# A gated linear-attention block and a 12-expert layer in one launch: the turn of x behind the turn of the keys in odd chunks, and five smaller edits of order and count

## The chip, the cores and the metric

The kernel runs on one core of one Trainium2 chip. The time is the device time of one execution in microseconds (us); the profile is of one execution of the same program on that core.

## What is computed

The reference, cut to what matters (the reshapes, the type conversions and the drawing of the inputs are left out):

```
# x: (1, 2048, 512) float32; 8 heads of 64
xn = layernorm(x, gamma, beta)
w = sigmoid(xn @ Wx @ Ww + bw); k = xn @ Wk; v = xn @ Wv; r = sigmoid(xn @ Wr)
for t in range(2048):                       # per head
    state = (1 - w[t])[:, None] * state + k[t][:, None] * v[t][None, :]
    y[t] = r[t] @ state
x = layernorm(x + y @ Wo)
p = softmax(x @ gate_w.T); top 2 of 12 experts, their weights made to sum to 1
x = layernorm(x + sum over the two experts of weight * (silu(x @ w1.T) * (x @ w3.T)) @ w2.T)
```

Every product of the dense layers is made of float16 high and low parts, three matmuls for one.

## The kernel before

Each engine runs an instruction list that is written out by hand; semaphores tie the lists together. There are two blocks, `attention` and `experts`.

**attention.** The 2048 tokens are 16 chunks of 128 (`NT`), two of which make a pair `q` (`NPAIR` = 8). The projections of a pair are ten jobs (`job` on TensorE, `take` on ScalarE): 0 and 1 turn the normalised x (line 358, eight transposes for both), 2 and 3 make the decay z, 4 and 5 the key, 6 and 7 the receptance, 8 and 9 the value. They share the two banks of `pA`, so job number i of `SEQUENCE` waits until take number i-2 is done. After the two takes of the turned x, ScalarE makes its float16 high part (`high_x`, line 794) and VectorE its low part (`low_x`, line 1055), and the jobs from 2 on need both.

Inside a chunk the recurrence is a tree of seven levels. For the chunk that comes next, VectorE multiplies the receptance side (`dve_level`, lines 715, 716 and 724) and POOL the key side (`pool_level`, line 740), while ScalarE copies the halves that stay (`act_receptance`, line 670, here `rec_levels`; `act_key`, line 683, here `key_levels`). Receptance level 6 on VectorE needs ScalarE's `rec_levels(5)`. For the present chunk TensorE makes `scores` half 0 (line 394), VectorE puts them through masks into `ST[0]` (`mask`, lines 1070 and 1073), and TensorE applies them to the values (`apply_values`, line 419); the same follows for half 1, where VectorE's `mask` half 1 stands behind levels 1 to 6 in its list. `read_state` (405) reads the carried state, `turn_keys` (429) turns the keys into `pM`, ScalarE copies that to `kbT` (902), and `attend_out` (454 to 456), the output projection of the chunk before, writes into the same `pM` and so waits for the copy.

Odd chunks 1 to 11 run with the slots `FIRST`, even ones from 2 on with `SECOND`, chunk 0 with `ZEROTH`. A `FIRST` chunk starts a new pair: ScalarE's `normalise` (800) makes the rows that jobs 0 and 1 turn. In TensorE's list its order is scores half 0, jobs 0 and 1, `read_state`, `turn_keys`, `attend_out`, `apply_values` half 0. In ScalarE's list it is `normalise`, the first levels, takes 0 and 1, the copy to `kbT`, `high_x`, further levels, `rec_levels(4)`, then `fill(0)`, the take of job 2, and behind it `rec_levels(5)`.

Beside all this the expert weights are split into float16 parts for the second block, in 48 pieces. `PIECES[n]` says how many are handled with the levels of chunk n, that is during chunk n-1: ScalarE makes the high part (`act_piece`, 691), POOL the low part (`pool_piece`, 746), and SP's queue moves them in and out through two buffers. The fourth piece of a chunk is the last thing in ScalarE's list of the chunk before, ahead of its `normalise`.

**The prologue** loads everything on SP's queue. TensorE runs six matmuls on a zeroed tile (572), then Wx @ Ww (576), the turns and the first jobs in the order of `START`. The weights of the output projection come last; ScalarE makes their high part in two halves (987, 1000) and POOL the low part (`low_out`, 1276), the second half behind the key levels of chunk 0.

**experts.** A routing part counts and ranks the tokens. In it TensorE keeps itself at work with matmuls on the identity (`busy`, line 1502), the last group of which has 21 and runs until VectorE has the routing tables and weights ready (line 1762). Then come 43 tiles of gathered tokens through `turn` (1537), `hidden` (1556 to 1558), `turn_hidden` (1564) and `down` (1574 to 1577), and a last part that adds and normalises.

## Time and profile before

| | |
|---|---|
| median of 3 runs | 780.29 us (778.42 to 787.46) |
| the profiled execution's own time | 779.44 us |
| its span, first to last instruction | 777.6 us |
| TensorE matmul busy | 736.8 us (95%), 6367 instructions |
| VectorE busy | 492.3 us (63%) |
| ScalarE busy | 347.4 us (45%) |
| POOL busy | 306.3 us (39%) |
| mean granted TensorE clock | 0.991 of full speed |

In the span, attention runs to about 460 us, routing to about 480 us, the tiles of the experts to about 744 us and the last part to the end. The rows further down are of four views. The waits say which engine an engine waited for. A timeline lists an engine's instructions in order of time: start, duration, engine, line, operation, output<-inputs, partitions and elements, how many were merged, and in square brackets the idle time before them with what ended it. A table of stretches gives busy time by engine with the clock. TensorE's matmuls overlap: in a merged row the last one's end is modelled and reaches about 0.16 us over the start of the next.

### The profile page before, as it was taken

The numbers are of one execution on the slowest core, as the hardware profiler recorded it, in microseconds if no ns is written. First come the engines' busy times: TensorE is split into PE (matmuls) and PEld (weight loads), VectorE is DVE, ScalarE is ACT, GpSimd is POOL, SyncE is SP. The second block draws the span as 40 slices with busy tenths as digits, with TensorE's granted clock in tenths as the row PEclk, the third lists the DMA queues.
The fourth block names the chain that finished last, engine by engine and source line by source line (L and its number), as shares of the span: only waits on it lengthen the run. The fifth ranks groups of instructions, "written<-read, shape, count | busy, mean of one in ns | idle before, by whom it ended". The sixth has DMA issues, their size and how long they took to land. (4 is left out here: it accounts for less than half of the span.)

```text
span 777.6 us, 18216 instructions
## 1 busy us (share of the span) xinstructions
PE 736.8 (95%) x6367; PEld 542.9 (70%) x6368; DVE 492.3 (63%) x1102; ACT 347.4 (45%) x695; POOL 306.3 (39%) x336
## 2 busy tenths in 40 slices
PE   9999899999999999999999988999999999999994
PEld 4778678787878777877867777666666666666641
DVE  3857868768586687785868876444444444444477
ACT  3865654556456566576465211222222222222264
POOL 0564555554554544655512002233443434334310
PEclk9999999999999999999999999999999999999998
DMA  9833455343552454537311026355355555532855
GB/s 333 295 101 118 142 184 164 113 158 112 184 179 74 163 164 146 172 124 236 112 43 41 28 74 235 141 203 188 131 217 217 211 198 200 189 94 81 326 231 199
DMA packets 40124, 126.79 MB, mean 163 GB/s; under 512 B 4224, under 2 KB 4608, under 8 KB 38144
## 3 DMA queue, kind: packets, MB, share of 16 engines
q1 hardware_dynamic: 31024, 99.49, 36.8%
q0 software_dynamic: 6880, 22.55, 8.6%
q10 hardware_dynamic: 2160, 3.93, 1.4%
q8 instruction: 40, 0.66, 0.4%
q14 instruction: 20, 0.16, 0.1%
HBM read 81.13 MB, written 44.83 MB: 162 GB/s over the span
## 5 line engine op out<-in xcount | busy, mean ns | idle before, releaser
L1070 DVE COPY_PREDICATED ST<-msk,pS 128x256 f32<-128x256 uint8 x224 | 121.2, 569 | 66.9 <-issue 37.7
L746 POOL TENSOR_TENSOR piece_parts<-piece,piece_parts 128x1024 f16<-128x1024 f32 x48 | 104.1, 2170 | 109.5 <-ACT piece_parts L691 109.5
L1556 PE MATMUL pH<-ring,xgh 128*128 x344 | 103.7, 301 | 3.9 <-issue 2.7
L740 POOL TENSOR_TENSOR L<-L,AM 128x256 f32<-128x256 f32 x96 | 73.0, 761 | 79.4 <-ACT L L683 70.9
L1557 PE MATMUL pH<-ring,xgh 128*128 x344 | 103.4, 301 | 0.0
L1558 PE MATMUL pH<-ring,xgl 128*128 x344 | 103.3, 300 | 0.0
L1868 POOL DMA_INDIRECT y_scratch<-ysb,sidx x43 | 42.9, 997 | 138.5 <-DVE ysb L1785 138.5
L394 PE MATMUL pS<-L 64*128 64x64 f32 x1536 | 96.2, 271 | 0.0
L1769 DVE TENSOR_TENSOR hid<-pH,sil 128x320 f32<-128x320 f32 x43 | 21.1, 492 | 118.3 <-ACT sil L1640 90.2
L394 PEld LDWEIGHTS pS<-L 64*128 64x128 f32 x1536 | 91.1, 188 | 0.0
L724 DVE TENSOR_TENSOR L<-L,AM 128x256 f32<-128x256 f32 x96 | 65.8, 686 | 26.2 <-ACT L L670 24.3
L1640 ACT ACTIVATE sil<-pH 128x320 f32<-128x320 f32 x43 | 18.8, 438 | 129.6 <-PE pH L1558 129.6
L369 PE MATMUL pA<-xh,early 128*128 128x256 f16 x256 | 69.8, 273 | 1.5 <-ACT val L788 1.1
L371 PE MATMUL pA<-xh,early 128*128 128x256 f16 x256 | 69.8, 273 | 0.0
L370 PE MATMUL pA<-xl,early 128*128 128x256 f16 x256 | 69.8, 273 | 0.0
L691 ACT CAST piece_parts<-piece 128x1024 f16<-128x1024 f32 x48 | 50.2, 1045 | 27.9 <-DMA piece<-in_w_experts 27.9
L1855 POOL DMA_INDIRECT xg<-x_scratch,gidx x39 | 39.0, 999 | 31.0 <-POOL gidx L1852 22.8
L1574 PE MATMUL pO<-ring,hTh 128*128 x129 | 49.0, 380 | 1.4 <-DVE hTh L1780 1.4
L1556 PEld LDWEIGHTS pH<-ring,xgh 128*128 128x128 f16 x344 | 33.7, 98 | 22.7 <-issue 10.0
L1636 ACT CAST hTh<-pHT 128x384 f16<-128x384 f32 x43 | 20.6, 479 | 63.4 <-PE pHT L1564 63.4
L1575 PE MATMUL pO<-ring,hTh 128*128 x129 | 48.9, 379 | 0.0
L1785 DVE COPY ysb<-pO 128x512 f32<-128x512 f32 x43 | 29.8, 692 | 22.9 <-PE pO L1575 20.4
(256 smaller groups left out, 1596.3 us busy)
## 6 DMA issues: line engine op xcount, KB each, us to landing
piece<-in_w_experts SPq DMA_DIRECT2D x48, 512.0 KB, 5.1
w_split_scratch<-piece_parts SPq DMA_DIRECT2D x48, 512.0 KB, 3.9
ring<-w_split_scratch SPq DMA_DIRECT2D x12, 2048.0 KB
yin<-y_scratch SPq DMA_DIRECT2D x16, 512.0 KB, 11.1
out_x<-X SPq DMA_DIRECT2D x8, 512.0 KB, 2.8
x_scratch<-X ACTq DMA_DIRECT2D x15, 256.0 KB, 2.0
X<-in_x SPq DMA_DIRECT2D x2, 1536.0 KB, 18.4
wxT_sb<-in_wxT SPq DMA_DIRECT2D x4, 256.0 KB, 4.9
```

The lines of the kernel that those rows point to most:

```text
L369: pe.matmul(o, wh[name][:, kt, cols], xh[par][:, kt, :], start=(kt == 0), stop=False)
L370: pe.matmul(o, wh[name][:, kt, cols], xl[par][:, kt, :], start=False, stop=False)
L371: i = pe.matmul(o, wl[name][:, kt, cols], xh[par][:, kt, :], start=False, stop=(kt == KT - 1))
L394: i = pe.matmul(o, k_, r_, start=True, stop=True)
L691: a.copy(piece_parts[buf][:, 0, :], piece[buf][:, :]).then_inc(piece_hi, 1)
L724: v.tensor_tensor(next_grown(k, lv, 1), grown(rec, k, lv, 1), factor(c, lv, 0), ALU.mult).then_inc(r_dec, 1)
L740: g.tensor_tensor(next_kept(k, lv, 0), kept(key, k, lv, 0), by, ALU.mult).then_inc(k_dec, 1)
L746: g.tensor_tensor(piece_parts[buf][:, 1, :], piece[buf][:, :], piece_parts[buf][:, 0, :], ALU.subtract).then_inc(piece_lo, 1)
L1070: v.copy_predicated(out[:, :, :, 0 if lv == 0 else 1, :], msk[:, lv, :, :].rearrange(shape, m=m), pS[:, :, lv * S:(lv + 1) * S].rearrange( ...
L1556: pe.matmul(p[:, 0, 0:F], xgh[par][:, k, :], wh, start=(k == 0), stop=False)
L1557: pe.matmul(p[:, 0, 0:F], xgh[par][:, k, :], wl, start=False, stop=False)
L1558: t = pe.matmul(p[:, 0, 0:F], xgl[par][:, k, :], wh, start=False, stop=(k == KT - 1))
```

## The change

There are six edits.

1. In `FIRST` chunks TensorE turns x (jobs 0 and 1) behind `read_state` and `turn_keys` instead of ahead of them, and ScalarE's takes 0 and 1 stand behind the copy to `kbT`.
2. In the same chunks ScalarE's `rec_levels(5)` stands ahead of `fill(0)`.
3. The zero matmuls at the start are 4 instead of 6.
4. The second half of the output weights' low part is made by VectorE behind chunk 0's receptance levels instead of by POOL behind its key levels; the semaphore `wo_lo` becomes two. In the prologue's ScalarE list `take(0, 8, 0)` stands two places further ahead.
5. `PIECES[1]` is 3 instead of 4 and `PIECES[5]` is 4 instead of 3.
6. The last `busy` of the routing part has 29 matmuls instead of 21.

```diff
@@ -51,7 +51,7 @@
 HALVES_OF = ((0, 1), (2, 3))
 GROUP = 4
 PIECE_AT = {4: (0,), 5: (1,), 6: (2, 3)}
-PIECES = [2, 4] + [4 if n % 2 == 0 else 3 for n in range(2, NT - 2)] + [0, 0]
+PIECES = [2, 3] + [4 if n % 2 == 0 or n == 5 else 3 for n in range(2, NT - 2)] + [0, 0]
 
 
 TOP = NL - 1
@@ -238,7 +238,7 @@
         y_out = sem("y_out")
         y_low = sem("y_low")
         wo_hi = sem("wo_hi")
-        wo_lo = sem("wo_lo")
+        wo_lo = [sem(f"wo_lo{i}") for i in range(2)]
         m_full = sem("m_full")
         kb_out = sem("kb_out")
         sd_ready = sem("sd_ready")
@@ -439,7 +439,8 @@
                 i.then_inc(m_full, 1)
 
             def attend_out(n):
-                pe.wait_ge(wo_lo, 2)
+                for i in range(2):
+                    pe.wait_ge(wo_lo[i], 1)
                 pe.wait_ge(y_out, n + 2)
                 pe.wait_ge(y_low, n + 2)
                 if n == NT - 1:
@@ -528,13 +529,13 @@
                 pe.wait_ge(k_dec, n * NL + (NL - 1))
                 pe.wait_ge(k_kept, n * (NL - 1) + (NL - 1))
                 scores(n, k, 0)
-                if slots is FIRST:
-                    job(q, 0, par)
-                    job(q, 1, par)
                 gating(0)
                 read_state(n, k)
                 if n < NT - 1:
                     turn_keys(n, k)
+                if slots is FIRST:
+                    job(q, 0, par)
+                    job(q, 1, par)
                 gating(1)
                 if slots is not FIRST:
                     fill(0)
@@ -568,7 +569,7 @@
                 fill(3)
 
             pe.wait_ge(zeroed, 1)
-            for i in range(6):
+            for i in range(4):
                 pe.matmul(pY[:, 0, :], state[:, 0, :], state[:, :, :].rearrange("p k t -> p (k t)"), start=True, stop=True)
             for kt in range(KT):
                 pe.wait_ge(wz_in[kt], 32)
@@ -762,7 +763,8 @@
                 bank, half = order(q, m) % 2, m % 2
                 a.wait_ge(a_full, order(q, m) + 1)
                 if q == 1 and (m == 6 or m == 8):
-                    a.wait_ge(wo_lo, 2)
+                    for i in range(2):
+                        a.wait_ge(wo_lo[i], 1)
                 if n is not None and m == 4:
                     a.wait_ge(s_full, n * 2 + 2)
                 if m < 2:
@@ -888,10 +890,7 @@
                 key_levels(0)
                 rec_levels(1)
                 key_levels(1)
-                if slots is FIRST:
-                    take(q, 0, par)
-                    take(q, 1, par)
-                else:
+                if slots is not FIRST:
                     early_norms()
                 if n == 0:
                     root(2, 7)
@@ -901,6 +900,8 @@
                     a.wait_ge(m_full, n * 3 + 1)
                     a.copy(kbT[:, :], pM[:, 0, :]).then_inc(kb_out, 1)
                 if slots is FIRST:
+                    take(q, 0, par)
+                    take(q, 1, par)
                     high_x(q, par)
                 if n == NT - 3:
                     a.wait_ge(x_lo, NPAIR)
@@ -931,11 +932,13 @@
                 split(0)
                 rec_levels(4)
                 if slots is FIRST:
+                    rec_levels(5)
                     if n == 9:
                         root_x1(0)
                     early_norms()
                     fill(0)
-                rec_levels(5)
+                else:
+                    rec_levels(5)
                 gating(4)
                 late_norms(4)
                 split(1)
@@ -1001,9 +1004,9 @@
             act_key(a, 0, 0, 0, 5)
             act_receptance(a, 0, 0, 1)
             act_receptance(a, 0, 0, 2)
+            take(0, 8, 0)
             act_receptance(a, 0, 0, 3)
             act_receptance(a, 0, 0, 4)
-            take(0, 8, 0)
             act_receptance(a, 0, 0, 5)
             act_piece(a, 0, 0, 0)
             take(1, 2, 1)
@@ -1248,6 +1251,8 @@
             dve_decays(v, 0, 0, 0)
             for lv in range(NL):
                 dve_level(v, 0, 0, 0, lv)
+            v.wait_ge(wo_hi, 2)
+            v.tensor_tensor(wo_l[:, 2:4, :], wo_stage[1], wo_h[:, 2:4, :], ALU.subtract).then_inc(wo_lo[1], 1)
             chunk(0, 0, nxt=0)
             for j in range((NPAIR - 2) // 2):
                 for u in range(2):
@@ -1271,10 +1276,6 @@
 
         @block.gpsimd
         def _(g):
-            def low_out(i):
-                g.wait_ge(wo_hi, i + 1)
-                g.tensor_tensor(wo_l[:, 2 * i:2 * i + 2, :], wo_stage[i], wo_h[:, 2 * i:2 * i + 2, :], ALU.subtract).then_inc(wo_lo, 1)
-
             g.wait_ge(stat1, 6)
             for i, name in ((1, "r"), (2, "v")):
                 g.wait_ge(w_hi, i + 1)
@@ -1283,9 +1284,9 @@
             for name in "krv":
                 g.wait_ge(w_lo[name], 1)
             g.wait_ge(wz_full, KT)
-            low_out(0)
+            g.wait_ge(wo_hi, 1)
+            g.tensor_tensor(wo_l[:, 0:2, :], wo_stage[0], wo_h[:, 0:2, :], ALU.subtract).then_inc(wo_lo[0], 1)
             pool_chunk(g, 0, 0, 0)
-            low_out(1)
             for t in range(PIECES[0]):
                 pool_piece(g, 0, 0, t)
             pool_chunk(g, 1, 1, 0)
@@ -1525,7 +1526,7 @@
             for n in range(NT, 2 * NT):
                 t = pe.matmul(pH1[:, 0, 0:SLOTS], ro.oh_col[:, n, :], oh_tile[:, n, :], start=(n == NT), stop=(n == 2 * NT - 1))
             t.then_inc(second_full, 1)
-            busy(21)
+            busy(29)
 
 
             def turn(i, k, rounds):
```

TensorE's list in a `FIRST` chunk, from the last scores of half 0 to the first of the output projection. The rows of before (358 is the turn of x, 405 `read_state`, 429 `turn_keys`, 454 to 456 `attend_out`):

```order
L394 MATMUL pS<-L 128x64 x12
L358 MATMUL pA<-idt,pair_x 128x128 x8
L405 MATMUL pY<-L,state 128x128 x4
L429 MATMUL pM<-idt,L 128x128 x4
L454 MATMUL pM<-wo_h,yTh 128x512
```

and of the changed kernel, where the output projection is line 455:

```order
L394 MATMUL pS<-L 128x64 x12
L405 MATMUL pY<-L,state 128x128 x4
L429 MATMUL pM<-idt,L 128x128 x4
L358 MATMUL pA<-idt,pair_x 128x128 x8
L455 MATMUL pM<-wo_h,yTh 128x512
```

The eight transposes of x have moved from ahead of the read to between the keys' turn and the output projection.

ScalarE's list in the first `FIRST` chunk, chunk 1, from a piece of the expert weights to the second take of z. The rows of before (800 is `normalise`, 773 the takes of x, 902 the copy to `kbT`, 794 the high part, 784 the takes of z, 670 the receptance levels, the last of which is `rec_levels(5)`):

```order
L691 CAST piece_parts<-piece 128x1024
L800 ACTIVATE pair_x<-X,nmr,rstd 128x512 x2
L683 COPY L<-key 128x256
L670 COPY L<-L 128x128x2
L683 COPY L<-L 128x128x2
L773 ACTIVATE pair_x<-pA,vecs 128x256 x4
L902 COPY kbT<-pM 128x512
L794 CAST xh<-pair_x 128x1024
...
L670 COPY L<-L 128x16x16
L784 ACTIVATE dec<-pA,neg_bw 128x2x128 x2
L670 COPY L<-L 128x4x2x32
```

and of the changed kernel (950 is the copy of y that stood ahead of the fourth piece before):

```order
L950 CAST yTh<-pY 128x512
L802 ACTIVATE pair_x<-X,nmr,rstd 128x512 x2
L684 COPY L<-key 128x256
L671 COPY L<-L 128x128x2
L684 COPY L<-L 128x128x2
L901 COPY kbT<-pM 128x512
L775 ACTIVATE pair_x<-pA,vecs 128x256 x4
L796 CAST xh<-pair_x 128x1024
...
L671 COPY L<-L 128x16x16
L671 COPY L<-L 128x4x2x32
L786 ACTIVATE dec<-pA,neg_bw 128x2x128 x2
```

The fourth piece is gone from ahead of `normalise`, the copy to `kbT` has passed the takes of x, and the last receptance copy has passed the take of z.

## Rows read from the trace of the kernel before

**Rows 1.** The waits of TensorE: line, who ended it, total, times, longest.

```profile
PE pM L454 <- ACT kbT L902: 5.6, 7, 1.2
PE pY L419 <- DVE ST L1073: 5.0, 11, 0.7
```

**Rows 2.** Timeline of TensorE in chunk 7, a steady odd chunk.

```profile
235.26 1.09 PE L358 MATMUL pA<-idt,pair_x 128*128 128x128 f32 x8
237.08 0.60 PE L429 MATMUL pM<-idt,L 128*128 128x128 f32 x4
238.50 0.38 PE L454 MATMUL pM<-wo_h,yTh 128*128 128x512 f16 x1 [0.82 <-ACT kbT L902]
...
241.19 0.66 PE L419 MATMUL pY<-ST,val 128*64 128x128 f32 x8
...
254.92 0.66 PE L419 MATMUL pY<-ST,val 128*64 128x128 f32 x8 [0.50 <-DVE ST L1073]
```

**Rows 3.** Timeline of VectorE in chunk 7.

```profile
240.03 0.42 DVE L1073 COPY ST<-pS 64x256 f32<-64x256 f32 x1
...
249.56 0.43 DVE L724 TENSOR_TENSOR L<-L,AM 128x256 f32<-128x256 f32 x1 [2.98 <-ACT L L670]
...
254.45 0.42 DVE L1073 COPY ST<-pS 64x256 f32<-64x256 f32 x1
```

**Rows 4.** Timeline of ScalarE in chunk 7.

```profile
235.95 1.93 ACT L773 ACTIVATE pair_x<-pA,vecs 128x256 f32<-128x256 f32 x4 [1.34 <-PE pA L358]
237.77 0.59 ACT L902 COPY kbT<-pM 128x512 f32<-128x512 f32 x1
238.23 1.07 ACT L794 CAST xh<-pair_x 128x1024 f16<-128x1024 f32 x1
```

**Rows 5.** Timeline of TensorE in chunk 1.

```profile
80.56 1.39 PE L358 MATMUL pA<-idt,pair_x 128*128 128x128 f32 x8 [1.94 <-ACT pair_x L800]
...
85.70 0.38 PE L454 MATMUL pM<-wo_h,yTh 128*128 128x512 f16 x1 [1.19 <-ACT kbT L902]
...
88.39 0.66 PE L419 MATMUL pY<-ST,val 128*64 128x128 f32 x8
```

**Rows 6.** Timelines of ScalarE, VectorE and POOL ahead of chunk 1's first mask.

```profile
77.95 1.04 ACT L691 CAST piece_parts<-piece 128x1024 f16<-128x1024 f32 x1 [2.42 <-DMA piece<-in_w_experts]
78.90 1.51 ACT L800 ACTIVATE pair_x<-X,nmr,rstd 128x512 f32<-128x512 f32 x2
...
79.47 2.02 DVE L715 TENSOR_TENSOR L<-rec,dec 128x256 f32<-128x256 f32 x1
81.41 1.06 DVE L716 TENSOR_TENSOR L<-rec,AM 128x256 f32<-128x256 f32 x1
...
79.07 2.14 POOL L746 TENSOR_TENSOR piece_parts<-piece,piece_parts 128x1024 f16<-128x1024 f32 x1 [2.48 <-ACT piece_parts L691]
```

**Rows 7.** Table of stretches: busy by engine, PEclk, DMA share, GB/s.

```profile
80.00:85.00 5.00, 3.95 (x20) 3.58 (x20) 4.71 (x6) 3.23 (x9) 3.61 (x4) 0.66 0.68 221
...
480.00:485.00 5.00, 5.00 (x28) 3.61 (x28) 0.69 (x1) 1.87 (x2) 0.00 (x0) 0.66 1.02 383
```

**Rows 8.** The page's DMA issues: KB each, median us to landing.

```profile
piece<-in_w_experts SPq DMA_DIRECT2D x48, 512.0 KB, 5.1
```

**Rows 9.** Timeline of TensorE in the prologue, first matmul of two runs of jobs.

```profile
30.68 0.27 PE L369 MATMUL pA<-xh,early 128*128 128x256 f16 x1 [0.35 <-ACT pair_x L773]
...
47.67 0.28 PE L369 MATMUL pA<-xh,early 128*128 128x256 f16 x1 [1.15 <-ACT val L788]
```

**Rows 10.** Timelines of ScalarE and POOL in the prologue.

```profile
34.78 0.84 ACT L784 ACTIVATE dec<-pA,neg_bw 128x256 f32<-128x256 f32 x2
...
44.11 2.31 POOL L1276 TENSOR_TENSOR wo_l<-rec,wo_h 128x1024 f16<-128x1024 f32 x1
```

**Rows 11.** Timeline of TensorE at the end of the routing part.

```profile
472.27 4.93 PE L1502 MATMUL pH<-idt 128*128 128x128 f32 x42
479.48 0.63 PE L1537 MATMUL pA<-idt,xg 128*128 128x128 f32 x4 [2.27 <-DVEq L1762]
```

## The prediction

> **What bounds the kernel now.** The table of the profile says that TensorE is busy for 95% of the span, so I looked for the few moments at which it is not. The waits of TensorE come first [rows 1]. 5.6 us in 7 waits stand ahead of the output projection and end with ScalarE's copy to kbT; 5.0 us in 11 waits stand ahead of applying the scores and end with VectorE's mask. Next I read the timeline of a steady odd chunk, chunk 7. There TensorE has two holes [rows 2]: 0.82 us ahead of line 454 and 0.50 us ahead of the second line 419. Chunks 3, 5, 9 and 11 repeat them, even chunks have neither. Then I read the other engines at these two places [rows 3, 4], and last the places where the holes are larger: chunk 1 [rows 5 to 7], the prologue [rows 9, 10] and the end of routing [rows 7, 11]. Everything between them is TensorE at full pace, which the change leaves as it is. So the sum is over holes.
>
> **Edit 1, the turn of x, in chunks 3, 5, 7, 9 and 11.** Before, ScalarE is in the takes of x from 235.95 for 1.93 us, to 237.88, and only then makes the copy to kbT [rows 4], although the keys' turn began at 237.08 and ended at 237.68 [rows 2]. TensorE starts line 454 at 238.50. In the new order TensorE reaches the keys' turn earlier by the turn of x: 1.09 us, less the overlap of 0.16, is 0.93. The keys' turn ends at 236.75, ScalarE is free, the copy takes 0.59 and is done at 237.4, while TensorE turns x until 237.6. Line 454 can start at about 237.55, which is 0.95 us earlier. All of it can't be kept: the next thing, line 419, needs VectorE's mask half 0, which starts when the scores are there, and those do not move. That mask ends at 240.03 + 0.42 = 240.45 [rows 3]; VectorE to TensorE takes 0.05 (254.87 to 254.92, [rows 2, 3]). So line 419 starts at 240.50 instead of 241.19: **0.69 us** a chunk. The bounds are 0 and 0.95.
>
> The takes of x are what is late now. They run from 237.35 to 239.3, the high part (1.07) to 240.2 or 240.3 instead of 239.30 [rows 4]. VectorE comes to the low part when the mask is done, at 240.37. The slack is 0.1 to 0.2 us; each 0.1 more would push levels 1 to 6 by 0.1. Behind `high_x` on ScalarE stand the key levels 2 and 3, for which POOL waits, and everything there comes about 0.9 us later. I cost this at nothing, since VectorE has a hole of 2.98 us before its last level [rows 3], which edit 2 opens.
>
> **Edit 2, `rec_levels(5)` ahead of the take of z.** VectorE's level 6 waited 2.98 us for a copy of 0.4 us that stood behind a take which waits for TensorE's z job. Now that copy follows `rec_levels(4)` directly; level 6 can run at about 247, when level 5 is done, and the mask of half 1 starts then instead of at 249.9. Even with 0.9 us lost to edit 1 it is done more than 1 us before TensorE comes to the second line 419. The hole of 0.50 goes: **0.57 us** with the overlap of 0.07 that adjacent matmuls have there. The bounds are 0 and 0.57.
>
> Five chunks at 0.69 + 0.57 = 1.26 are **6.3 us**.
>
> **Chunk 1, edits 1, 2 and 5.** Here ScalarE waits 2.42 us for the transfer of a fourth piece and splits it, then normalises x from 78.90 on [rows 6], and TensorE sits 1.94 us ahead of the turn of x [rows 5]. The same piece on POOL, 79.07 to 81.21, stretches VectorE's level 0 to 2.02 + 1.06 us; elsewhere these two take 0.42 each, pitched 0.33, so VectorE is ready for the mask at 82.47 instead of about 80.2. On top of that the granted clock falls: 0.66 over 80 to 85 [rows 7], and the turn of x takes 1.39 instead of 1.09 [rows 2, 5]. Without the piece normalise is done before TensorE asks. VectorE then bounds the chunk: level 0 ready at 80.2 (in the times of before), 4.9 us of mask (249.97 to 254.87 in chunk 7, [rows 3]), 0.3 left for POOL's first key level beside it, and line 419 at about 85.45 instead of 88.39. That is **2.9 us**, and 0.55 for the second mask as above, **3.5 us**. TensorE still sits about 0.8 us twice in it, which is less than either idle time after which the clock fell. Bounds: 1.9 (the wait for normalise alone) and 4.5: from the end of the scores, 80.56 - 1.94 = 78.62, to line 419 it is 9.77 us here, and would be 240.50 - 235.26 = 5.24 in a steady chunk [rows 2, 5].
>
> **The rule for two engines at one memory.** VectorE's line 715 starts at 79.47, POOL's piece ends at 81.21, and line 715 ends at 81.49 [rows 6]: not slowed but held until the piece is through. The Trainium skill, "SBUF — State Buffer", section "Who interferes with whom", says this: a VectorE instruction with two inputs in SBUF and a GpSimd instruction share one port pair, the first to start has it to its end, and the other waits in full. The trace agrees, with 0.28 us between the two ends.
>
> That speaks against edit 5, since chunk 5 now has the fourth piece. There the load is issued once the second piece is through, takes 5.1 us [rows 8], and POOL's work of 2.14 us falls on the same level 0. Chunk 4 has the even chunk's longer lead, and I find level 0 ready for chunk 5's mask within 0.2 us of the scores: **-0.2 us**, bounds 0 and -3.
>
> **Prologue, edits 3 and 4.** TensorE sits 1.15 us at 47.67 for the take of the value [rows 9], 1.31 with the overlap of 0.16. That take stood behind receptance copies which VectorE delayed, and VectorE was held by POOL's second half of the low part, 44.11 to 46.42 [rows 10]. Both are moved: the take comes two copies earlier, and the low part (about 1.2 us on VectorE, like the low part of x of the same size) falls between the levels and the mask, where VectorE has nothing to do. All **1.3 us** come back; bounds 0 and 1.3. Two zero matmuls fewer are 1.7 us at the pace of the last ones, but it does not last: job (0, 6), the third of the run from 30.68, needs the take (0, 2), which ends at 34.78 + 0.84 = 35.62 [rows 9, 10] behind a cast that waits for the transfer of the output weights. TensorE came there at about 35.9. So **0.3 us**, bounds 0 and 1.7.
>
> **End of routing, edit 6.** 42 records in 4.93 us are 0.117 each [rows 11]; a matmul is two, so 8 more are 1.9 us, inside the hole of 2.27. They delay nothing, 0.4 us of idle stays. The gain is the clock: after the hole it was 0.66 over 480 to 485 [rows 7]. At 1.2 instead of 2.4 GHz for part of the stretch, 5 x (1 - 0.66) = 1.7 us are lost; some 0.4 of it falls on fill matmuls that hide behind ScalarE's and VectorE's parts of the first tile. **1.3 us**, bounds 0 and 1.7.
>
> **The sum.** 6.3 + 3.5 - 0.2 + 1.3 + 0.3 + 1.3 = 12.5 us. From the profiled execution's 779.44 that gives 766.9, say **767.0 us**, and a span near 765.1. The median of the three runs is 0.85 above the profiled execution, within their own scatter.
>
> **Rivals.**
>
> *The odd chunks keep their second hole.* POOL's pieces, later by 0.9 us, hold VectorE's levels, or the late high part of x does, and the mask of half 1 ends no earlier than TensorE's arrival. Against it: 2.98 us of room. For it: the slack of 0.1 to 0.2 at the low part. Six chunks lose 0.57: 767.0 + 3.4 = 770.4.
>
> *The fourth piece does in chunk 5 what it did in chunk 1.* For it: the same two instructions meet, and a level 0 that is held until the piece is through passes its whole delay to the mask. Against it: a transfer that starts earlier against TensorE. It costs up to 3 us and perhaps the clock: 770 to 771. (By the rule of the Trainium skill, "SBUF — State Buffer", section "Who interferes with whom", POOL's piece would be first here and VectorE held in full; the hold in rows 6 agrees.)
>
> *The turns uncover a wait, and it is slower.* Before, the turn of x gave 0.93 us between the scores and the read of the state and the keys' turn. If the last key level of POOL or the state were that late, TensorE would sit in each odd chunk. To be slower at all this must cost more than 12.5 / 6 = 2.1 us a chunk; at 2.5 it would be 782. Against it: in even chunks the read follows the scores directly, and line 405 has no entry among TensorE's waits.
>
> *The gains don't add, no change.* If the masks of half 0 alone bounded the odd chunks and moved with the copies on ScalarE, edits 1 and 2 would give nothing, and 12.5 - 6.9 = 5.6 us would be left: 773.8.
>
> **How the numbers follow.** The forecast has 0.60; either of the first two rivals 0.22; no change in the odd chunks 0.09; the slower one 0.03; 3 us more than forecast (VectorE freer in chunk 1 than I count, the prologue at its bound) 0.06. The range reaches from 763.5 (chunk 1 and the prologue at their upper bounds) to 771.5, which takes in the first two rivals. 1% is 7.8 us, about what a measurement of this kernel can tell: faster than 772.5 us 0.86, within 1% 0.11, slower 0.03; 0.02 of the first two rivals I count within 1%, for the scatter.
>
> **What would show it.** In the changed profile TensorE's waits for kbT should fall from 5.6 us in 7 to under 1.5 us, in chunks 1 and 14 alone; line 419's first application in each odd chunk should follow the mask's copy by 0.05 us with a hole near 0.1, the second should have none; VectorE's hole of 2.98 ahead of level 6 should be gone; the clock should read 1.0 in chunk 1 and after routing; the wait at 47.67 should be gone, and one of up to 1.1 us should appear ahead of job (0, 6). The prediction is wrong if `low_x` waits for the high part by more than 0.3 us, if chunk 5 shows a late mask, or if the clock falls at a place where it did not before.

## The result and the profile after

The changed kernel takes 774.71 us, the median of 13 runs (771.47 to 777.42); beside it on the same chip the kernel before takes 780.29 us (778.05 to 787.46, 13 runs). The ratio is 0.9914, with a 95% interval of 0.9887 to 0.9941. So it is faster, by 0.9%, where 1.7% was forecast, and the time is outside the range. The profiled execution took 777.42 us with a span of 775.5 and was the slowest of the 13; the profiled execution of before, 779.44, was one of its better ones (4 of its 13 runs were faster). That matters below.

The waits of TensorE in the changed kernel, to be read against [rows 1] (line 455 is the output projection, 405 the state's read):

```profile
PE pY L419 <- DVE ST L1076: 3.3, 7, 0.9
PE pY L405 <- issue: 2.2, 1, 2.2
PE pA L369 <- ACT dec L786: 1.8, 1, 1.8
...
PE pM L455 <- DVE yTl L1192: 1.0, 1, 1.0
...
PE pA L1538 <- DVEq L1763: 0.5, 1, 0.5
...
PE pM L455 <- ACT kbT L901: 0.3, 1, 0.3
```

The 5.6 us for kbT are 0.3, those for the mask 3.3 instead of 5.0. Two waits are new: 2.2 us ahead of the state's read and 1.8 ahead of a job. (The 1.0 us for yTl, the low part of y, is at the end of chunk 15, where the kernel before has a wait of 1.0 us at its line 501.)

Chunk 7 in the changed kernel, TensorE, against [rows 2]:

```profile
230.31 1.16 PE L405 MATMUL pY<-L,state 128*128 128x128 f32 x8
231.31 0.60 PE L429 MATMUL pM<-idt,L 128*128 128x128 f32 x4
231.74 1.04 PE L358 MATMUL pA<-idt,pair_x 128*128 128x128 f32 x8
232.67 0.38 PE L455 MATMUL pM<-wo_h,yTh 128*128 128x512 f16 x1
...
235.63 0.62 PE L419 MATMUL pY<-ST,val 128*64 128x128 f32 x7 [0.21 <-DVE ST L1076]
...
248.80 0.44 PE L419 MATMUL pY<-ST,val 128*64 128x128 f32 x4
```

VectorE and ScalarE beside it, against [rows 3, 4]:

```profile
235.07 0.42 DVE L1076 COPY ST<-pS 64x256 f32<-64x256 f32 x1
235.47 1.23 DVE L1058 TENSOR_TENSOR xl<-pair_x,xh 128x1024 f16<-128x1024 f32 x1
...
240.75 2.15 DVE L725 TENSOR_TENSOR L<-L,AM 128x256 f32<-128x256 f32 x2
242.83 4.49 DVE L1073 COPY_PREDICATED ST<-msk,pS 128x256 f32<-128x256 uint8 x7
...
231.94 0.59 ACT L901 COPY kbT<-pM 128x512 f32<-128x512 f32 x1 [2.29 <-PE pM L429]
232.43 1.94 ACT L775 ACTIVATE pair_x<-pA,vecs 128x256 f32<-128x256 f32 x4
234.39 1.04 ACT L796 CAST xh<-pair_x 128x1024 f16<-128x1024 f32 x1
```

The copy to kbT now waits for TensorE, not for the takes, and TensorE goes into line 455 with no hole. The high part of x ends at 235.43, the mask at 235.49: VectorE comes to the low part 0.06 us after it is there. Level 6 follows level 5 directly (two in 2.15), the idle time of 2.98 us is gone, and the second line 419 has no hole. In chunk 7 everything stands as forecast, but for 0.21 us instead of about 0.1 ahead of the first line 419.

The stretches make it plain where the program stands. The numbers are us from the first scores of a chunk to those of another, from the timelines of TensorE, in the two profiles and in a second profile of each kernel (the experiments tell of them); the first row and the last are a time from the span's start and the whole span:

```
                               before   changed   changed, 2nd   before, 2nd
first scores of chunk 0         53.02     51.59       51.83          53.73
chunk 1                         30.55     29.09       28.23          32.09
chunks 3, 5, 7, 9, 11          133.31    128.14      127.86         133.31
chunks 13 and 14                46.51     48.15       46.51          46.51
chunk 15 to the routing part    31.31     37.00       37.00          36.44
first to second tile of x        6.54      5.45        5.45           6.49
span                            777.6     775.5       773.2          786.6
```

Up to chunk 13 the changed kernel is 8.0 us ahead (384.39 against 376.40). Then it loses 1.6 us in chunks 13 and 14 and 5.7 in chunk 15, where the two programs are the same instruction by instruction. The stretches of the changed kernel show why (columns as in [rows 7]):

```profile
100.00:390.00 290.00, 287.05 (x3044) 229.84 (x3042) 220.01 (x398) 173.37 (x348) 151.49 (x124) 1.00 0.48 154
390.00:400.00 10.00, 10.00 (x96) 8.52 (x94) 7.38 (x15) 4.80 (x11) 1.46 (x2) 0.83 0.16 58
400.00:430.00 30.00, 28.77 (x330) 22.15 (x329) 23.91 (x91) 15.38 (x36) 4.06 (x6) 1.00 0.10 37
430.00:456.00 26.00, 24.11 (x188) 21.59 (x187) 16.25 (x63) 3.61 (x9) 0.00 (x0) 0.74 0.06 21
```

The granted clock, 1.00 over the 290 us of steady chunks, was at its lower level (1.2 GHz) for part of 390 to 400 and for half of 430 to 456. So 7.3 us went to the clock in a part of the program that the change doesn't touch.

### The profile page after: what moved, and what is told of

It reads as the page before. It is cut to its first block and busy times, and to the rows that moved or that the text cites. A ratio compares the mean times of both kernels' runs of the same rounds, so it can differ in the third digit from the quotient of the medians.

```text
span 775.5 us, 18242 instructions
## 1 busy us (share of the span) xinstructions
PE 742.6 (96%) x6379; PEld 551.1 (71%) x6380; DVE 501.4 (65%) x1103; ACT 347.9 (45%) x695; POOL 302.5 (39%) x335
## 5 line engine op out<-in xcount | busy, mean ns | idle before, releaser
L741 POOL TENSOR_TENSOR L<-L,AM 128x256 f32<-128x256 f32 x96 | 70.7, 736 | 84.1 <-ACT L L684 75.2
L394 PE MATMUL pS<-L 64*128 64x64 f32 x1536 | 98.8, 276 | 0.0
L394 PEld LDWEIGHTS pS<-L 64*128 64x128 f32 x1536 | 93.6, 193 | 0.0
L725 DVE TENSOR_TENSOR L<-L,AM 128x256 f32<-128x256 f32 x96 | 68.7, 716 | 11.3 <-ACT L L671 9.4
```

The source lines that it names most:

```text
L394: i = pe.matmul(o, k_, r_, start=True, stop=True)
L741: g.tensor_tensor(next_kept(k, lv, 0), kept(key, k, lv, 0), by, ALU.mult).then_inc(k_dec, 1)
```

## The experiments

The theories. **A**: the holes (idle times of TensorE) were worth what the trace up to chunk 13 shows; the clock falls at places that differ from one execution to the next, in either kernel, and one profile of each happened to differ. **B**: moving the turns makes the clock fall later on. **C**: the holes of 0.70 and 0.91 us in chunks 14 and 15 make it fall. **D**: the places belong to the instruction lists, and came with the change.

**The changed kernel again**, no edit.

> The changed kernel itself, a second time. Theory A (the clock falls at places that differ from one execution to the next, in either kernel): its profile shows low clock at other places than the first profile (chunk 1, chunks 13 and 15, the end), and its times spread over 5 us or more with the mean clock. Theory D (the places belong to the instruction lists): the same stretches again. At a like mean clock it should be some 8 us below the kernel before.

Measured: 774.59 us (772.58 to 777.24, 7 runs) against 784.08 us (23 runs of before on that chip), ratio 0.9893 (0.9854 to 0.9932). Its profile:

```profile
74.00:90.00 16.00, 13.10 (x169) 10.97 (x168) 14.50 (x25) 11.10 (x25) 7.08 (x7) 1.00 0.26 90
...
390.00:400.00 10.00, 10.00 (x111) 7.98 (x110) 7.91 (x23) 5.89 (x12) 1.04 (x2) 1.00 0.22 80
...
430.00:456.00 26.00, 24.11 (x188) 21.68 (x186) 16.00 (x66) 3.17 (x8) 0.00 (x0) 0.74 0.06 21
```

The clock held in chunk 1 and in chunk 13, where it had fallen in the first profile of the same program, and fell in chunk 15 again. With the clock held chunk 1 takes 28.23 us instead of 29.09. The times spread over 4.7 us, a little less than A asked for.

**The kernel before again**, no edit.

> The kernel before, profiled a second time. Theory A: its first profile, at a mean clock of 0.991 and 779.44 us, was one of its better executions, and an execution of ordinary clock (0.984 to 0.986) shows stretches of low clock in the gating chunks 13 to 15 as the changed kernel does, with an end 4 to 6 us later than 779.4. Theory D (the low clock in chunks 13 to 15 came with the change): nothing under 1.0 between 85 and 460 us, and about 779.

Measured: 788.41 us at a mean clock of 0.978 (one execution), and in its profile:

```profile
74.00:90.00 16.00, 12.05 (x106) 8.62 (x105) 14.92 (x24) 10.87 (x22) 8.74 (x7) 0.79 0.60 189
100.00:390.00 290.00, 282.90 (x3016) 227.51 (x3015) 212.90 (x395) 165.81 (x332) 151.69 (x121) 1.00 0.47 152
390.00:440.00 50.00, 47.62 (x505) 35.98 (x504) 39.07 (x125) 28.93 (x65) 7.95 (x12) 1.00 0.10 38
440.00:465.00 25.00, 23.62 (x183) 20.95 (x182) 15.56 (x62) 3.18 (x8) 0.00 (x0) 0.73 0.06 22
465.00:480.00 15.00, 13.53 (x110) 12.35 (x108) 11.73 (x49) 2.07 (x3) 0.00 (x0) 0.89 0.43 159
```

The kernel before loses the clock in chunk 15 too (36.44 us to the routing part, against 37.00 in the changed kernel), and also in the routing part, where neither profile of the changed kernel does. This is one execution, 9.0 us above the profiled one on which the prediction was built, where 4 to 6 were expected, and it settles D: the low clock of chunk 15 did not come with the change. Of the 14 profiles of all kernels here, the clock held all through chunk 15 in two (31.3 and 31.7 us to the routing part), it was low for 3.4 us in three (31.7 to 32.3), and for 6.8 to 13.7 us in nine (33.8 to 37.0). In eight of these nine, kernels of either order among them, it fell 14 to 16 us behind the chunk's first scores. So A is right in that no execution need have the fall, but the place is not at random: chunk 15 is where it comes most. In chunk 13 it fell in one profile of the 14, the first of the changed kernel.

**A measure at a like clock.** Every run has its mean granted clock. In the 60 runs of before that stood beside the experiments it goes from 0.977 to 0.994, and the time from 788.92 to 776.87 with it. One slope fits all kernels, 0.59 us for 0.001 of mean clock (fitted within kernels). With it each kernel's mean is put at a clock of 0.985:

```
                                runs   mean clock   mean us   at 0.985   error
before                            60      0.9851     783.46     783.5     0.1
changed (first chip)              13      0.9855     774.79     775.1     0.3
changed, again                     7      0.9867     774.72     775.7     0.5
edits 1 and 2 alone                4      0.9892     773.58     776.1     0.3
edit 1 alone                      10      0.9906     777.17     780.5     0.3
edit 2 alone                      10      0.9870     779.11     780.3     0.3
edits 3 to 6 alone                10      0.9860     782.49     783.1     0.2
changed, pieces as before         10      0.9847     776.94     776.8     0.3
changed, six zero matmuls          9      0.9868     774.84     775.9     0.2
changed, pad before chunk 13       5      0.9858     775.41     775.9     0.5
changed, late fill                 4      0.9872     773.68     775.0     0.5
changed, low y ahead               4      0.9885     773.65     775.7     0.3
low y ahead, six zero, late fill   6      0.9932     770.50     775.3     0.4
```

At a like clock the change is worth 7.8 us beside the runs of before of the same chip, and 8.4 by the runs of the first chip; the runs of before that stood beside those have no clock on record. The last column is the scatter of the runs alone. The correction is a fit, and a fall of the clock doesn't cost the same everywhere: 3.4 us at the lower level in chunk 15 made the way to the routing part 0.4, 0.5 and 1.0 us longer in three profiles. It also takes the mean clock as given, which an edit could itself move. Where a trace has the stretch itself, I use the trace.

**Edits 1 and 2 alone.**

```diff
                 scores(n, k, 0)
-                if slots is FIRST:
-                    job(q, 0, par)
-                    job(q, 1, par)
                 gating(0)
                 read_state(n, k)
                 if n < NT - 1:
                     turn_keys(n, k)
+                if slots is FIRST:
+                    job(q, 0, par)
+                    job(q, 1, par)
                 gating(1)
```

(with the takes and `rec_levels(5)` moved as in the change)

> The kernel before with the two edits of order alone (turn of x behind the keys' turn, last receptance copy ahead of the take of z). In the trace of the changed kernel the five odd chunks 3 to 11 gave 1.17, 0.87, 1.16, 0.81 and 1.06 us, 5.1 together, and chunk 1 may give 0.5 to 1 more. Theory A (the holes are worth what the trace shows, and what is missing in the whole is the clock of chunks 13 and 15, which depends on when the program comes to them): attention reaches the start of chunk 13 about 5.5 us earlier than before; the time is 773.5 to 775 if the clock holds in chunks 13 to 15 and up to 8 us more if it falls. Theory B (moving the turns makes TensorE's later work itself slower, wherever it lies): the clock falls in chunks 13 and 15 at the same instructions as in the changed kernel.

Measured: 772.44 us (771.01 to 778.42, 4 runs) against 784.17 (14 runs), ratio 0.9881 (0.9828 to 0.9933). In the trace the five steady odd chunks take 25.48 to 25.50 each, against 26.66: 1.17 us a chunk, 5.9 in all. Chunk 1 takes 29.10. At a like clock 7.4 of the 7.8 us are here. Attention reaches chunk 13 at 377.47, 6.9 us before the first profile of before, where 5.5 were expected. B would have the clock fall where it did in the changed kernel; it held in chunk 13 and fell for 3.4 us in chunk 15, later in the chunk.

**Edits 3 to 6 alone** (the changed kernel with the order taken back).

> The changed kernel with the two edits of order taken back: prologue, pieces and routing fill alone. Theory A: chunk 0 starts 1.4 us earlier, chunk 1 gives about 1.5 more, the routing fill 1.1; with the clock held in chunks 13 to 15 that is 775 to 776, up to 8 us more if it falls. Theory B: the clock never falls in chunks 13 to 15, since the turns are where they were.

Measured: 782.85 us (777.86 to 784.98, 10 runs) against 784.17 (14 runs), ratio 0.9990 (0.9961 to 1.0019), so no gain can be told from none. B falls here: with the turns in their old place the clock fell in chunk 15 all the same (36.95 us to the routing part). The prologue's gain was lost in this profile: TensorE waited 2.23 us ahead of job (0, 6), the clock was low over 36 to 40 us, and chunk 0 started at 53.76, no earlier than before. At a like clock the four edits together give 0.4 us, with an error of 0.2: much less than the 2 to 3 us that the prologue, chunk 1 and the first tile show together in the traces of the changed kernel. The experiment on the pieces, below, shows a part of the reason.

**Edit 1 alone.**

> The kernel before with the turn of x moved behind the keys' turn, alone. In the trace: TensorE's wait for kbT in the steady odd chunks goes from 0.82 us to nothing, a hole of 0.1 to 0.2 us stands ahead of line 419's first application, and the second hole of 0.5 us stays, since level 6 is still behind the take of z: 0.6 to 0.7 us less for each of the chunks 3 to 11. At a like clock 4 to 5 us below the kernel before.

Measured: 777.22 us (774.65 to 779.83, 10 runs) against 782.84 (23 runs), ratio 0.9930 (0.9896 to 0.9964). The steady odd chunks take 26.04 to 26.08 us: 0.61 less. The trace has the hole ahead of the first application that was expected:

```profile
139.97 0.66 PE L419 MATMUL pY<-ST,val 128*64 128x128 f32 x8 [0.21 <-DVE ST L1072]
```

Chunk 1 gains nothing by this edit alone: it takes 31.27 us, with a hole of 3.17 us ahead of the state's read and a fall of the clock at it.

**Edit 2 alone.** `rec_levels(5)` ahead of `fill(0)` in the kernel before.

> The kernel before with the last receptance copy ahead of the take of z, alone. In the trace: VectorE's idle time of 3 us ahead of level 6 goes, and TensorE's hole of 0.5 us ahead of line 419's second application with it: 0.57 us less for each of six odd chunks, the wait for kbT stays at 0.82. At a like clock 3 to 3.5 us below the kernel before.

Measured: 777.14 us (776.24 to 785.04, 10 runs) against 782.84 (23 runs), ratio 0.9945 (0.9905 to 0.9984). The steady odd chunks take 26.09 or 26.10 us: 0.56 less. In the steady odd chunks the two edits add up, 0.61 + 0.56 = 1.17, as in the kernel with both. At a like clock they are 3.0 us, where 4 to 5 were expected, and 3.2: together 6.2, against 7.4 for the kernel with both. In the traces the missing 1.2 us are chunk 1, which takes 31.27 us with edit 1 alone, 30.41 with edit 2 alone and 29.10 with both, against 30.55 and 32.09 before.

**A pad ahead of chunk 13.**

```diff
+                if n == NT - 3:
+                    pe.wait_ge(s_dve, n * 2 + 1)
+                    busy(pS[:, 0, :], 4)
                 scores(n, k, 0)
```

> The changed kernel with 4 more matmuls on the identity ahead of chunk 13's scores, 0.94 us; they change nothing before, and in chunks 13 to 15 only when the same work is done. Theory A (time of arrival): the stretches of low clock in chunks 13 and 15 move to other instructions, shrink, or go; total between 5 us faster and 3 us slower than the changed kernel. Theory B: they stay at the same instructions, and the time is the changed kernel's plus 0.9.

Measured: 777.04 us (771.15 to 777.87, 5 runs), ratio 0.9884 (0.9842 to 0.9926). The clock was low for 6.8 us in chunk 1, held in chunk 13, fell in chunk 15 (36.95 us to the routing part) and in the routing part (18.46 us instead of 17.25). Since the unpadded kernel held in chunk 13 too in its second profile, this says nothing of the moment of arrival: the experiment doesn't decide what picks the execution in which the clock falls.

**The late fills.**

```diff
                 gating(5)
+                if n == NT - 2:
+                    pe.wait_ge(gate_out, 18)
+                    busy(pA[:, 1, :], 3)
...
-                    busy(pA[:, 0, :], 10)
+                    busy(pA[:, 0, :], 14)
```

> The changed kernel with TensorE's holes late in chunk 14 and early in chunk 15 (0.70 and 0.91 us) filled by 3 and 4 more matmuls on the identity. If those holes make the clock fall behind them (theory C: less work just before the fall decides), the low stretch of 13.7 us in chunk 15 goes and the time falls by about 6 us to some 769 to 770. Theory A: it may stay or go, with no loss of more than 0.3 us from the fill itself.

Measured: 773.87 us (770.95 to 776.01, 4 runs), ratio 0.9883 (0.9843 to 0.9922). The profile held the clock in chunk 15, at a time of 770.95. But the other three runs have mean clocks of 0.983, 0.988 and 0.985, like the changed kernel's. C isn't shown; at a like clock the kernel is within the errors of the changed one (775.0), so the fill costs nothing that can be told.

**The pieces as before.**

```diff
-PIECES = [2, 3] + [4 if n % 2 == 0 or n == 5 else 3 for n in range(2, NT - 2)] + [0, 0]
+PIECES = [2, 4] + [4 if n % 2 == 0 else 3 for n in range(2, NT - 2)] + [0, 0]
```

> The changed kernel with the pieces as before, 4 for chunk 1 and 3 for chunk 5. If the fourth piece cost chunk 1 what I said, chunk 1 is longer by about 2 us again (TensorE waits for normalise or for the mask); chunk 5 is shorter by 0.3 us (25.8 against 25.5 in the trace). Rival: chunk 1 is bound by VectorE's decays and low part of y (the hole of 2.2 us ahead of line 405), and the piece, being behind them, costs under 0.5 us.

Measured: 777.19 us (770.81 to 781.5, 10 runs), ratio 0.9918 (0.9881 to 0.9956). Chunk 1 takes 31.23 us, 2.1 to 3.0 more than in the changed kernel, with a hole of 3.20 us ahead of the state's read. Its clock was low for 6.9 us, so the fair neighbour is the profile of the pad, the changed kernel up to there, with 6.8 us of low clock in chunk 1 and 30.32 us for it: 0.9 us. At a like clock the times say 1.1 to 1.7. The piece was not behind the decays, as the rival had it: on POOL from 77.32 to 79.48 us, it falls on the last decay, which takes 1.98 us instead of 0.17 and holds back the low part of y. Chunk 5 takes 25.50, against 25.78 and 25.51 in the two profiles of the changed kernel: its fourth piece costs 0 to 0.3 us. What the second rival said of its mechanism came true in the first of them, for VectorE's level 0 is held by the piece, but the mask was late by 0.3 us only:

```profile
177.62 2.22 DVE L716 TENSOR_TENSOR L<-rec,dec 128x256 f32<-128x256 f32 x1
...
177.42 2.14 POOL L747 TENSOR_TENSOR piece_parts<-piece,piece_parts 128x1024 f16<-128x1024 f32 x1 [2.67 <-ACT piece_parts L692]
...
185.86 0.66 PE L419 MATMUL pY<-ST,val 128*64 128x128 f32 x8 [0.51 <-DVE ST L1076]
```

Edit 5 is worth its place beside edits 3 and 4. Without them it may be worth little: with four pieces and the old prologue (edits 1 and 2 alone) chunk 1 ends at 104.32 us; with four pieces and the new prologue it starts 1.8 us earlier and ends at 104.68. So the prologue's gain is lost again in chunk 1 unless the piece goes. This is one profile of each, and their clocks in chunk 1 differ.

**The low part of y ahead of the decays.**

```diff
-                if n:
+                if n and ((n - 1) % 2 or n - 1 >= NT - 2):
                     low_y(n - 1)
...
+                if n % 2 == 0 and n < NT - 2:
+                    low_y(n)
                 if k % 2 == 0 and n < NT - 2:
                     dve_decays(v, n + 2, nxt + 1, in_pair(k + 2)[0])
```

> The changed kernel with the low part of y at the end of even chunks ahead of VectorE's decays instead of behind them. If the hole of 2.2 us ahead of the state's read in chunk 1 is the low part of y waiting behind 4.9 us of decays, it goes to under 0.3 us, the clock holds in chunk 1, and at a like clock elsewhere the kernel is 1 to 2.5 us faster than the changed one; chunk 1 stays bound by its mask, so the hole moves in part to line 419. Rival: the hole only moves, and nothing is gained but the clock.

Measured: 774.75 us (769.7 to 775.38, 4 runs), ratio 0.9881 (0.9819 to 0.9942). The expectation had 1 to 2.5 us at a like clock. TensorE's waits, and its rows in chunk 1:

```profile
PE pY L419 <- DVE ST L1076: 4.5, 9, 0.9
...
PE pM L455 <- ACT kbT L901: 1.8, 3, 1.2
```

```profile
76.96 1.16 PE L405 MATMUL pY<-L,state 128*128 128x128 f32 x8
77.96 0.60 PE L429 MATMUL pM<-idt,L 128*128 128x128 f32 x4
78.40 1.04 PE L358 MATMUL pA<-idt,pair_x 128*128 128x128 f32 x8
80.67 0.38 PE L455 MATMUL pM<-wo_h,yTh 128*128 128x512 f16 x1 [1.24 <-ACT kbT L901]
...
84.28 0.66 PE L419 MATMUL pY<-ST,val 128*64 128x128 f32 x8 [0.86 <-DVE ST L1076]
```

The hole of 2.2 us ahead of line 405 is gone, and 1.24 and 0.86 us stand further on: ScalarE's copies wait for level 0, and the mask bounds the chunk. Chunk 1 takes 27.48 us, 0.75 less than the changed kernel with its clock held. The cause of the new wait is shown. But it is no gain: chunk 5, where TensorE now waits 0.83 us for the mask, takes 26.11 us and chunk 10 takes 24.71, against 25.51 and 24.28 in the changed kernel's second profile. From the first scores of chunk 0 to those of chunk 13 it is 323.85 us, against 323.57 there. At a like clock both are at 775.7. The rival that was named beforehand holds: nothing is gained but, where it would fall in chunk 1, the clock.

**Six zero matmuls.**

> The changed kernel with six zero matmuls again. The hole ahead of job (0, 6), 1.8 us in the changed kernel, shrinks to about 0.1 us, chunk 0 starts at most 0.3 us later, and the clock can't fall in the prologue. So it is the same within 0.3 us at a like clock, or faster where the changed kernel's clock falls there (as in the run with the order taken back, at 36 to 39 us).

Measured: 775.41 us (771.72 to 778.68, 9 runs), ratio 0.9907 (0.9874 to 0.9939). The hole ahead of job (0, 6) is 0.82 us instead of 1.55 and 1.79, and not the 0.1 that was expected. Chunk 0 starts at 51.91 instead of 51.59 and 51.83: by these profiles edit 3 is worth 0.1 to 0.3 us, and 775.9 against 775.7 at a like clock doesn't contradict it. The profiles scatter by more, though: in the four other kernels with four zero matmuls and the new prologue, whose clock held there, the hole is 0.96 to 1.72 us and chunk 0 starts at 51.27 to 51.94.

**All together**: low y ahead, six zero matmuls, the two late fills, on the changed kernel.

> The changed kernel with the low part of y ahead of the decays, six zero matmuls, and the two late fills of chunks 14 and 15. From the runs so far: chunk 1 0.7 us shorter with the clock held and 1.6 shorter where it fell, the prologue without a long hole. At a like clock 1 us below the changed kernel; if fewer long holes make falls of the clock rarer (mean clock 0.989 instead of 0.986) a median of 772 to 773 instead of 774.7. If the fills and the prologue don't matter, it is the low_y kernel, 774 to 775.

Measured: 770.56 us (768.4 to 773.22, 6 runs) against 782.84 (23 runs), ratio 0.9836 (0.9786 to 0.9887). It is faster than the kernel before, and 4 us below the changed kernel's two medians, which were not taken beside it. At a like clock it is where the changed kernel is (775.3 against 775.7), not 1 us below; what it has is the clock, 0.990 to 0.996 in six runs with a mean of 0.993, against 0.983 to 0.994 and a mean of 0.986 in the changed kernel's 20. It has no hole over 1.3 us between chunk 0 and chunk 13, and none over 0.4 in the prologue. Which of the three edits keeps the clock isn't separated, and that fewer holes are the reason isn't shown either: on the same chip the ten runs of edit 1 alone, with a hole of 3.17 us in chunk 1, have a mean clock of 0.991.

## Why the prediction was wrong, step by step

**The holes, and that the rest would stay as it is.** Right up to chunk 13: even chunks take 24.28 us in the profiles of both kernels, but for chunk 10 of the changed kernel's first, 24.39. The steady odd chunks were forecast to give 0.69 + 0.57 = 1.26 each and gave 1.17 (0.61 + 0.56 when taken apart). The 0.09 are in the first term, the mask of half 0. The mask was given 5.24 us from the first matmul behind the scores to line 419 and has 5.32 (230.31 to 235.63), of which VectorE's last copy to line 419 takes 0.14 instead of the 0.05 that I read off the other mask. In chunk 9 the mask has an idle moment of 0.5 us of its own and the chunk gives 0.80; that one I did not see coming, and its cause stays open. With edits 1 and 2 alone chunk 9 gives 1.17, and with the pieces as before it gives 0.82, so it takes the new order and edit 3 or 4. Five chunks: 6.3 forecast, 5.2 and 5.4 in the two profiles.

**Chunk 1.** Forecast 3.5, measured 1.5 with the clock lost again and 2.3 with it held. The step that failed is "VectorE then bounds the chunk" at line 419 alone. I let TensorE go into the state's read at the end of the scores. But that read overwrites the bank from which VectorE makes the low part of y, and the low part stands behind VectorE's decays. The trace of before had it already, 0.93 us behind the end of the scores at 78.62:

```profile
78.86 0.69 DVE L1189 TENSOR_TENSOR yTl<-pY,yTh 128x512 f16<-128x512 f32 x1
```

In the changed kernel:

```profile
73.54 2.28 DVE L707 TENSOR_TENSOR AM<-dec 128x512 f32<-128x512 f32 x1
75.86 2.40 DVE L707 TENSOR_TENSOR AM<-AM 128x256 f32<-128x256 f32 x5
78.29 0.17 DVE L707 TENSOR_TENSOR dec_end<-AM 128x8 f32<-128x8 f32 x1
78.48 0.69 DVE L1192 TENSOR_TENSOR yTl<-pY,yTh 128x512 f16<-128x512 f32 x1
...
73.15 2.13 POOL L747 TENSOR_TENSOR piece_parts<-piece,piece_parts 128x1024 f16<-128x1024 f32 x1 [2.71 <-ACT piece_parts L692]
75.24 1.29 POOL L741 TENSOR_TENSOR L<-key,dec 128x256 f32<-128x256 f32 x1
```

```profile
79.39 1.19 PE L405 MATMUL pY<-L,state 128*128 128x128 f32 x8 [2.22 <-issue]
80.37 1.06 PE L429 MATMUL pM<-idt,L 128*128 128x128 f32 x4
81.23 1.91 PE L358 MATMUL pA<-idt,pair_x 128*128 128x128 f32 x8
```

TensorE starts the read at 79.39, 0.22 us behind the low part's end. In the kernel before the turn of x and the wait for `normalise` covered this. It is the third rival, a wait that the moved turns uncover; I had priced it only for all odd chunks and judged it by even ones, in which the low part of y has no decays ahead of it. It stands in chunk 1 alone. There VectorE comes to the decays 0.16 us behind the chunk's first scores (73.38); in chunk 5 it comes 3.2 us ahead of them, and a first decay that is held as long (1.96 us) costs nothing. In chunk 1 the third piece holds the first decay, 2.28 us to 75.82 where it takes 0.69 when nothing is beside it. And with the fourth piece gone, POOL's first key level, for which I had left 0.3 us, falls on the next decays, which take 2.40 us instead of the 1.45 of before. So level 0 begins 5.7 us behind the chunk's first scores, instead of the 4.6 of before from which I counted. (The Trainium skill, "SBUF — State Buffer", section "Who interferes with whom", says that a VectorE instruction with two inputs in SBUF is blocked in full until POOL's ends, where POOL's was first. The first decay and the piece agree: POOL's runs from 73.15 to 75.28, the decay from 73.54 to 75.82.)

**The clock in chunk 1** was counted as regained because the idle times would be "less than either idle time after which the clock fell". The hole was 2.2 us, and the clock fell in the first profile (the turn of x took 1.91 us instead of 1.04) and held in the second, behind a hole of 2.51 us.

**The prologue.** Forecast 1.3 + 0.3, measured 1.43 and 1.19 against the first profile of before; against its second (53.73) and three other kernels with the old prologue (53.43 to 53.72), 1.6 to 2.1. The wait at 47.67 is gone, and the new wait is where it was foretold, 1.79 us instead of at most 1.1. Job (0, 6) starts at 35.81 instead of 35.91, so the fewer zero matmuls gave 0.1 of their 0.3 us in this pair of profiles:

```profile
35.81 0.27 PE L369 MATMUL pA<-xh,wh_r 128*128 128x256 f16 x1 [1.79 <-ACT dec L786]
```

**The end of routing.** Forecast 1.3 for the clock. The fill is as costed, 58 records in 6.72 us, and 0.48 us of the hole stay, where I had 0.4:

```profile
471.60 6.72 PE L1503 MATMUL pH<-idt 128*128 128x128 f32 x58
478.80 0.63 PE L1538 MATMUL pA<-idt,xg 128*128 128x128 f32 x4 [0.48 <-DVEq L1763]
...
484.25 0.60 PE L1538 MATMUL pA<-idt,xg 128*128 128x128 f32 x4
```

The first tile takes 5.45 us instead of 6.54, so 1.1 us. But with edits 1 and 2 alone and with edit 1 alone, which have the old fill, it took 5.45 and 5.44 too, behind the same hole of 2.26 us. The edit takes away a loss that some executions have, three of the five profiles with the old fill and none of the nine with the new.

**What the sum was made against.** This is the other step that failed. The forecast took 12.5 us from 779.44, the time of one execution, and treated its falls of the clock, in chunk 1 and after routing, as the only ones and as tied to their places. I said that the median was above it "within their own scatter", and did not ask what the scatter was. It was the clock: before runs at 0.977 to 0.994, its profiled execution at 0.991. The profile of the changed kernel drew a fall in chunk 13 and the long one in chunk 15, 7.3 us. The first profile of before had been spared both; its second had the long one too. At a like clock the terms come to 7.8 us instead of 12.5: about 1 was too much in the odd chunks, 1.2 to 2.0 in chunk 1, and most of what I counted for the clock in chunk 1 and after routing is not had in an ordinary execution, because the clock falls there or elsewhere anyhow (this last part is what is left of the difference, not a measurement). Put at a like clock, the forecast's 767.0 misses by 4.7 us in its terms (12.5 - 7.8) and by 4.1 in its base (783.5 - 779.44); that makes 775.8 us, and the 13 measured runs are at 775.1 at that clock.

**The rivals and the signs.** The second hole of the odd chunks did not stay. Chunk 5 kept its fourth piece for 0 to 0.3 us. The uncovered wait came, in one chunk. The fourth rival's 773.8 us is nearest to the measured 774.71, by luck: it had the odd chunks give nothing, and they gave 5.2 to 5.4 us. Of the three signs of being wrong the clock is the plain one: it fell in chunks 13 and 15, where it had not before. `low_x` waited 0.64 us for the high part, in chunk 1 of the first profile alone, and chunk 5's mask was late by 0.3 us there. None of my four cases held the measured time for its reason; I had no case for "the gains come, and the clock takes part of them back elsewhere".

## What to carry to other kernels

Where a kernel's runs spread by more than the effect that is sought, ask first what spreads them: one number for each run, here the mean granted clock, went with most of a spread of 12 us, and one profile of each kernel, the slowest run of one against a better run of the other, hid 6 us of an 8 us gain. When an engine is let into an instruction earlier, look at every semaphore of what now comes first, one by one, in the chunk with the latest producers and not in a steady one. When a wait is taken away in one chunk, measure over the chunks behind it too: the low part of y gave 0.75 us in chunk 1 and nothing by chunk 13. And an edit of order between a copy and a take that waits is cheap to find: an idle time on one engine that ends with a 0.4 us copy on another stood for half of the gain.

## What the runs showed of the hardware

TensorE's granted clock fell from 1.00 to 0.50 (2.4 to 1.2 GHz) without a long idle time ahead of it. In chunk 15 of the changed kernel these rows come ahead of the stretch at the lower level, which began in the scores at 438.46; the longest idle time of the 14 us before is 0.91 us:

```profile
436.88 0.66 PE L419 MATMUL pY<-ST,val 128*64 128x128 f32 x8 [0.91 <-DVE ST L1076]
437.47 1.06 PE L483 MATMUL pA<-gw,pair_x 128*128 128x12 f32 x8
438.46 0.33 PE L394 MATMUL pS<-rec,key 64*128 64x64 f32 x2
```

The engine was busy for 24.11 of the 26 us of that stretch, with transposes, scores of 64 columns and gate products of 12, and the clock was low for half of them. Between 100 and 390 us, where projections stand between the scores, it fell in none of the 14 profiles. TensorE's matmuls were the same in both kernels for the 42 us ahead of the fall at 394 us, to 0.01 us from matmul to matmul, and so they were in the changed kernel's second profile; the clock fell in the first profile of the changed kernel and held in the others, so what TensorE does just before does not decide alone. And an idle time of 2.2 to 2.5 us was followed by a fall in some executions (2.22 us in chunk 1 of the changed kernel) and not in others (2.51 us in its second profile).
